# V's high and low parts in one stationary tile, and the halves of each head's output added afterwards

## What is computed

```python
def attention(x, ctx, Wq, Wk, Wv, Wo, bo):
    q = (x @ Wq).reshape(b, n, HEADS, D_HEAD)
    k = (ctx @ Wk).reshape(b, m, HEADS, D_HEAD)
    v = (ctx @ Wv).reshape(b, m, HEADS, D_HEAD)
    sim = jnp.einsum('bihd,bjhd->bhij', q, k) * SCALE
    attn = jax.nn.softmax(sim, axis=-1)
    out = jnp.einsum('bhij,bjhd->bihd', attn, v).reshape(b, n, HEADS * D_HEAD)
    return out @ Wo + bo

h = layernorm(x, ln1_g, ln1_b)
x = attention(h, h, a1_Wq, a1_Wk, a1_Wv, a1_Wo, a1_bo) + x
h = layernorm(x, ln2_g, ln2_b)
x = attention(h, context, a2_Wq, a2_Wk, a2_Wv, a2_Wo, a2_bo) + x
```

## Time and profile before

| | us |
|---|---|
| median of 3 runs | 1088.36 |
| lowest and highest | 1087.58, 1089.52 |
| the profiled execution | 1088.15 |
| its span in the trace | 1086.4 |
| one self-attention batch of 8 steps | 51.72 |
| one cross-attention batch of 8 steps | 37.76 |

### The profile page before, as it was taken

The page is one execution under the profiler, slowest core; times in us unless marked ns, Lnnn a source line. Parts: engine busy times, 40 slices in busy tenths (PEclk is TensorE's granted clock), DMA queues, the critical chain, the costliest instruction groups (busy, mean ns, idle before and its releaser), DMA issues.

```text
span 1086.4 us, 21327 instructions
## 1 busy us (share of the span) xinstructions
PE 997.5 (92%) x7872; PEld 937.3 (86%) x7872; DVE 710.9 (65%) x1598; ACT 626.5 (58%) x1945; POOL 357.2 (33%) x474
## 2 busy tenths in 40 slices
PE   5688874599999999999999999999999998899998
PEld 4577753489999999899999899999999997899998
DVE  4466744596766676667667775666677667566664
ACT  3466452386656575657566765666666666533333
POOL 1101324033334333333333244454554454401010
PEclk9999887699999999999999998999999999999999
DMA  6221000100200000000000300300000001010100
GB/s 205 68 68 39 20 20 20 44 11 2 98 2 21 1 21 1 21 1 21 2 21 3 101 25 1 103 25 2 25 26 18 8 21 46 17 38 21 40 30 21
DMA packets 28121, 34.62 MB, mean 32 GB/s; under 512 B 2164, under 2 KB 21364, under 8 KB 28020
## 3 DMA queue, kind: packets, MB, share of 16 engines
q1 hardware_dynamic: 28020, 33.26, 9.9%
HBM read 24.86 MB, written 8.39 MB: 31 GB/s over the span
## 4 chain that ended last, share of the span: by engine, by line
PE 79%; DVE 10%; ACT 6%; issue 2%; POOL 1%; DMA 1%; SPq 1%; DVEq 0%; POOLq 0%
PE bank L1306 17%; PE bank L1307 16%; PE bank L1308 16%; PE bank L1523 8%; PE bank L1506 5%; PE bank L1564 3%; PE bank L1565 3%; PE bank L1566 3%; PE bank L1538 3%; ACT p L721 1%; PE bank L1480 1%; PE bank L1414 1%; DVE bn L887 1%; PE bank L1415 1%; PE bank L1416 1%
## 5 line engine op out<-in xcount | busy, mean ns | idle before, releaser
L721 ACT ACTIVATE p<-bank,negmax 128x256 f32<-128x256 f32 (+1 forms) x512 | 208.2, 428 | 18.0 <-DVE negmax L1088 15.1
L538 POOL TENSOR_TENSOR oT_hi<-oT,ones 128x256 fp32r<-128x256 f32 x128 | 94.0, 735 | 378.0 <-DVE oT L1111 378.0
L731 ACT CAST pT_hi<-bank 128x512 fp32r<-128x512 f32 (+1 forms) x256 | 110.7, 485 | 166.1 <-PE bank L1523 165.3
L1306 PE MATMUL bank<-hT_hi,w_hi 128*128 128x256 f32 x640 | 190.6, 298 | 5.9 <-DVE hT_lo L1072 2.5
L1308 PE MATMUL bank<-hT_hi,w_lo 128*128 128x256 f32 x640 | 181.5, 284 | 0.0
L1307 PE MATMUL bank<-hT_lo,w_hi 128*128 128x256 f32 x640 | 181.3, 283 | 0.0
L1306 PEld LDWEIGHTS bank<-hT_hi,w_hi 128*128 128x128 f32 x640 | 122.6, 192 | 9.2 <-DVE hT_lo L1072 4.8
L1103 DVE TENSOR_TENSOR pT_lo<-bank,pT_hi 128x512 fp32r<-128x512 f32 (+1 forms) x256 | 129.7, 548 | 0.3
L1084 DVE TENSOR_REDUCE negmax<-bank 128x2 f32<-128x512 f32 x128 | 82.2, 684 | 66.8 <-PE bank L1506 66.8
L1307 PEld LDWEIGHTS bank<-hT_lo,w_hi 128*128 128x128 f32 x640 | 122.9, 192 | 0.0
L1308 PEld LDWEIGHTS bank<-hT_hi,w_lo 128*128 128x128 f32 x640 | 122.6, 192 | 0.0
(11 more groups left out here) (200 smaller groups left out, 2787.2 us busy)
## 6 DMA issues: line engine op xcount, KB each, us to landing
w_stage<-in_weights SPq DMA_DIRECT2D x52, 256.0 KB, 4.8
x_in<-x_dram SPq DMA_DIRECT2D x24, 256.0 KB, 2.9
x_dram<-x_out SPq DMA_DIRECT2D x16, 256.0 KB, 3.2
l_x<-in_x SPq DMA_DIRECT2D x4, 512.0 KB, 5.6
x_dram<-l_out SPq DMA_DIRECT2D x4, 512.0 KB, 2.9
out_dram<-x_out SPq DMA_DIRECT2D x8, 256.0 KB, 3.1
l_ctx<-in_ctx SPq DMA_DIRECT2D x4, 240.0 KB, 5.3
ctx_in<-in_ctx SPq DMA_DIRECT2D x8, 120.0 KB, 3.2
```

The lines of the kernel that those rows point to most:

```text
L538: nc.gpsimd.tensor_tensor(oh[:, G % PAIRS, :], of[:, :], ones[:, :], ALU.mult).then_inc(y["o_hi"], 1)
L721: last = nc.scalar.activation(p[:, G % 2, e, t * cols:(t + 1) * cols], scores_at(G, e, t), ACT.Exp, bias=negmax[:, G % 2, t, e:e + 1], acc ...
L731: nc.scalar.copy(pTh[0:r, G % 2, e, 0:n], bank[4 + e][0:r, 0:n]).then_inc(y["pT_hi"], 1)
L1306: nc.tensor.matmul(dst, lh, rh, start=(i == 0), stop=False)
```

## The change

- V is stored as [head 0 high, low, head 1 low, high] for each pair, 64 columns each (`VW = 2 * DH`, one tile `v_hi_lo` in place of two with zeros). One stationary tile of 128 columns then holds both parts of one head, and a matmul with p's high part and one with p's low part give all four products. Each head has its own half of bank 6, with the products of V high in one half of the partitions and those of V low in the other. So there are 8 matmuls a pair in self-attention (12 before) and 4 in cross-attention (6 before). The sixteen memsets of the zero columns go.
- The two halves of the partitions have to be added: ScalarE copies the low halves out of PSUM (`copy_low_values`, two copies of 64x256), VectorE adds them to the high halves (`add_low_values`, two additions of 64x256). The product with the reciprocals moves to GpSimd, ahead of `split_o`'s two instructions.
- The transposes of `rsum_wide` no longer have room in bank 6. They go to bank 3 at the end of each of TensorE's steps (`transpose_sums`). Bank 3 is also the head projection's, so they wait until that has been rounded (`qk_lo` or `v_lo`), and the next head projection waits for ScalarE's copy of them (`rT_copied`). ScalarE makes that copy at the start of its next step.

```diff
-VW = 3 * DH
+VW = 2 * DH
...
             def split_o(G):
+                pool.wait_ge(y["o_sum"], G + 1)
+                pool.wait_ge(y["rT_copied"], G + 1)
+                if G >= 1:
+                    pool.wait_ge(y["o_lo"], G)
+                nc.gpsimd.tensor_tensor(on[:, :], of[:, G % 2, :], rT[:, G % 2, :], ALU.mult).then_inc(y["o_norm"], 1)
                 pool.wait_ge(y["o_norm"], G + 1)
...
             def copy_rT(G):
+                act.wait_ge(y["rT"], G + 1)
+                if G >= 2:
+                    act.wait_ge(y["o_norm"], G - 1)
+                nc.scalar.copy(rT[:, G % 2, :], bank[3][:, 0:S]).then_inc(y["rT_copied"], 1)
+
+            def copy_low_values(G):
+
                 act.wait_ge(y["o"], G + 1)
-                nc.scalar.copy(rT[:, :], bank[6][:, S:2 * S]).then_inc(y["rT_copied"], 1)
+                nc.scalar.copy(ob[0:DH, :], bank[6][DH:128, 0:S])
+                nc.scalar.copy(ob[DH:128, :], bank[6][0:DH, S:2 * S]).then_inc(y["o_low"], 1)
...
-            def normalise_o(G):
-                dve.wait_ge(y["rT_copied"], G + 1)
-                if G >= 1:
-                    dve.wait_ge(y["o_lo"], G)
-                nc.vector.tensor_tensor(of[:, :], bank[6][:, 0:S], rT[:, :], ALU.mult).then_inc(y["o_norm"], 1)
+            def add_low_values(G):
+                dve.wait_ge(y["o_low"], G + 1)
+                if G >= 2:
+                    dve.wait_ge(y["o_norm"], G - 1)
+                nc.vector.tensor_tensor(of[0:DH, G % 2, :], bank[6][0:DH, 0:S], ob[0:DH, :], ALU.add)
+                nc.vector.tensor_tensor(of[DH:128, G % 2, :], bank[6][DH:128, S:2 * S], ob[DH:128, :], ALU.add
+                                        ).then_inc(y["o_sum"], 1)
...
-            for v_ in (vh, vl):
-                for pr in range(PAIRS):
-                    last = nc.vector.memset(v_[:, :, pr * VW + DH:pr * VW + 2 * DH].bitcast(F32), 0.0)
-            last.then_inc(zeros_ready, 1)
...
+            def transpose_sums(G):
+                pe.wait_ge(y["rsum_wide"], G + 1)
+                for t in range(NT):
+                    last = nc.tensor.transpose(bank[3][:, t * 128:(t + 1) * 128], rsw[:, G % 2, t, :], ident[:, :])
+                last.then_inc(y["rT"], 1)
...
                 if G >= 1:
-                    pe.wait_ge(y["o_norm"], G)
-                for t in range(NT):
-                    nc.tensor.transpose(bank[6][:, S + t * 128:S + (t + 1) * 128], rsw[:, G % 2, t, :], ident[:, :])
...
-                product(bank[6][:, 0:S], terms).then_inc(y["o"], 1)
+                for e in range(2):
+                    dst = bank[6][:, e * S:(e + 1) * S]
+                    for j in range(tiles):
+                        vs = vv[0:r, j, (2 * g + e) * VW:(2 * g + e + 1) * VW]
+                        pc = slice(j * S, (j + 1) * S)
+                        nc.tensor.matmul(dst, vs, pTh[0:r, G % 2, e, pc], start=(j == 0), stop=False)
+                        last = nc.tensor.matmul(dst, vs, pTl[0:r, G % 2, e, pc], start=False, stop=(j == tiles - 1))
+                last.then_inc(y["o"], 1)
...
                     project_out(b, 0, 3)
+                if i <= 4:
+                    pe.wait_ge(y["qk_lo"], products_until(b, i + 3))
+                elif not turn:
+                    pe.wait_ge(y["qk_lo"], products_until(b + 1, i - 5))
...
+                transpose_sums(G)
...
+                if i == 0:
+                    pe.wait_ge(y["qk_lo"], key_product(b, 1))
+                if i in (1, 2):
+                    pe.wait_ge(y["qk_lo"], query_product(b, i + 1))
+                if i == 3:
+                    pe.wait_ge(y["v_lo"], value_product(b, 1))
+                if i in (5, 6) and more:
+                    pe.wait_ge(y["qk_lo"], query_product(b + 1, i - 5))
+                transpose_sums(G)
```

64 lines of the change are left out of this document (35 added, 29 removed).

## The result

The changed kernel takes 1123.24 us (median of 4 runs, 1117.01 to 1129.71) against 1088.72 for the kernel before, a ratio of 1.0318 (95% interval 1.0272 to 1.0365). It is 34.5 us slower; the forecast was 1109, within 1093 to 1127. The profiled execution is the longest of the four runs: 1129.71, with a span of 1127.9 and a mean granted clock of 0.947 (0.969 before).

A forecast was written before the change was run, and what follows sets the result against it. TensorE's own work bounded the kernel; new waits on the rounding chain would outweigh the matmuls saved. Self -8.5 +3 +1, cross +16.8 +2 +3.7, clock +2.5 gave a 1107 span, forecast 1109 us, range 1093 to 1127.

The forecast's parts named there:

- rival 1: TensorE's clock: two to four more stretches at half clock, since stops recur in each cross batch; 1117 to 1127; chance 0.22.
- the forecast case: Whole kernel: waits at step ends outweigh the removed matmuls, 1093 to 1114 with the waits' uncertainty; chance 0.58.
- plus 0.37: End of self steps: 0.15 us until TensorE goes on plus 0.22 for two transposes, added to the chain.
- the sum: Self and cross batch gains and losses, +18 us on a span of 1086.4, plus 2.5 for the clock: 1107.
- 0 on the path: Extra ScalarE and VectorE instructions: no time added to the steps, except on ScalarE in cross i = 5.
- the upper bound of 0.76 a step: ScalarE's extra work from the two copies and the moved reciprocals' copy: at most 0.76 us a step.
- the lower bound of 0.27: ScalarE's extra work if the reciprocals' copy only takes another queue place: at least 0.27 us a step.
- Rival 2: Chain shorter than read in 48 steps: 0.4 us less each cancels the loss, 0.6 gives about 1080; chance 0.11.
- Rival 3: New waits cost nothing: all 48.8 us of TensorE's removed matmuls come off, 1040; chance 0.02.
- Rival 4: GpSimd becomes late: 0.5 us in the 24 cross steps TensorE sets, 12 us more, 1121; chance 0.03.

The follow-up runs named there:

- the combined version: The changed kernel with ScalarE's rounding reordered (self steps), reciprocals in bank 4, x_plus_bias moved and V's rounding earlier (cross steps): 1121.20 us; with stops filled, 1093.05 us.
- the run with the same count: The changed kernel with its removed matmuls put back as overwritten repeats, 12 a self step and 6 a cross step: 1150.62 us.
- the run with the extra work: The kernel before with the change's extra ScalarE, VectorE and GpSimd instructions in cross steps, results unused, no wait added: 1129.57 us, ratio 1.0382.

## Why the prediction was right, and where its sizes were off

**The sign and the mechanism held.** The new wait sets the step, and the step is the chain through ScalarE and VectorE plus what stands behind it. The wait alone costs 18 us and the fewer matmuls bring 22 (by the profiled spans; 27 by the medians), not 48.8. Of the sixteen step lengths of a self and a cross batch, fifteen came out within 0.1 us of the working. The conditions that I gave for being wrong (a self batch that gains over 2.5, a cross batch that loses under 1) did not occur. The range held the time only because it took in rival 1: the forecast case ended at 1114, and the forecast of 1109 was 14 under.

**Three runs put in a row.** The wait added to the kernel before makes 18.1 us. From there to the changed kernel with the old count of matmuls it is 44.7 more (1150.62 - 1105.96), and taking the matmuls away gives 27.4 back (35.4 together; 34.5 was measured against the first runs of the kernel before). So the largest part is neither the wait by itself nor the matmuls, but what comes with the change besides them: the two transposes behind the wait, the other engines' instructions, and the clock. By stretches of the two profiles, 4.8 of it is in six middle self batches (i = 2 and 3, 0.37 each, which I read as the transposes), 12.3 in the steps of six middle cross batches (1.22 a batch in i = 3, where `hT_lo` takes 1.05 longer), 9.6 in half clock there, and 18 in the first and last batches of the stages and the ends of the kernel.

**The steps of self-attention.** i = 4 to 6 were to be 6.07 and are 6.13, i = 2 was to be 6.08 and is 6.13, i = 3 6.70 and is 6.76. The term "plus 0.37" is 0.43 (388.27 to 388.70 and 401.16 to 401.59 above): a gain of 5.9 in six batches in place of 8.5.

**The steps of cross-attention.** i = 0 came to 6.75 (6.72), i = 2 to 4.65 (4.63), i = 4 to 4.94 (4.95), i = 5 to 5.17 (5.18). The term that was mis-sized is i = 3: 6.33, not 5.73, which makes 3.6 us in six batches. The step of the argument that failed is the one on GpSimd. I asked of its third instruction only whether `rsum_wide` would be late, and found 0. `rsum_wide` ends 3.71 after the scores' start in i = 3, 0.28 after TensorE's own work, but V's low part comes later still. `x_plus_bias`, however, the next in GpSimd's queue, now starts 0.08 us ahead of VectorE's `hT_lo`, not 0.76, and `hT_lo` takes 1.74 us where it had taken 1.08. Where the two don't meet it takes 0.69, and the step is 5.28.

**The first and the last batches.** The first self batch lost 5.4 (3 expected), the last one 3.4 (1), the part after the middle cross batches 7.1 (3.7). Before the first step there are 1.9 that I hadn't counted. The first cross batch gained 0.8 where I had +2, since most of its half clock fell away. In the first self batch the wait alone costs 3.7. In the last cross batch a part is clock: from 955 to 965 us it was at half, where it was full in the two rows of the kernel before above. The rest of these sums I haven't taken apart:

```profile
955.00:960.00 5.00, 3.25 (x16) 2.95 (x15) 3.09 (x6) 3.89 (x13) 2.44 (x4) 0.50 0.30 101
```

With the clock below, all these terms make up the 21 us by which the profiled span is over the sum (41.5 for 20.5): 2.6 and 3.7 in the middle batches, 9.9 in their clock, 2.4 + 2.4 + 1.9 + 3.4 at the ends, less 2.8 in the first cross batch and the 2.5 set down for the clock.

**The clock.** I took 2.5 us, for none or one more stretch of half clock, and gave two to four more a chance of 0.22. Four of the six middle cross batches show it, for 9.9 us in the profiled execution. So what happened is the forecast's mechanism together with rival 1, and the median, 1123.2, lies in that rival's range. My reason against it, that stops of this size were few in the trace, says only that the trace couldn't tell. The rows of the last cross batch, with three stops of 2.25 and one short fall of the clock, leave it open too; but the stop recurs in every cross batch, and that should have weighed more.

**The other engines.** "0 on the path" for ScalarE and VectorE holds in the middle batches of the changed kernel, but, as I read it, for a reason that I didn't see: the wait holds TensorE back to their pace, so that the extra work finds room. Without the wait the same work makes i = 4 late by 1.2 us in the kernel before, and a cross batch of the combined version stays 2.1 over before even with its stops filled; half clock comes on top of both. ScalarE's two copies do not stand in place of another: the reciprocals' copy only moved, and a cross batch has 6.1 us more on ScalarE (30.96 for 24.88), which is the upper bound of 0.76 a step; no run shows the lower bound of 0.27. Rival 2 (a shorter chain) didn't come by itself; when ScalarE's order was changed it did, for 18 us. Rival 3 is refuted by the run with the same count. Rival 4 as I had put it, for the 24 cross steps that TensorE sets, is refuted by the waits: `rsum_wide` ended only four, three of them in the last cross batch.

**What stays open.** Why, of the six stops of 2.7 us in the middle cross batches, two were followed by 3.9 and 4.1 us of loss, two by about 1 us and two by none, while the stop of 2.08 in the run with the extra work was followed by half clock each time, and the kernel before kept full clock behind two of its stops of 2.24 and 2.25.

## What to carry to other kernels

A trade that takes work from the busiest engine is worth what its shortened steps can use: compute for each step the chain that the new wait adds, and for each other engine what stands behind the new work in its queue. It may pay in one stage and lose in the next; here self-attention alone, with ScalarE's order changed, turned 3.2% slower into 1.5% faster. Price a stop of TensorE twice, by its length and by the clock after it, and if it can't be avoided, filling it with unused products may be worth more than it costs.
